# The second feed-forward stage token by token: its convolution as three shifted float32 products

## The reference, cut to what matters

```python
def act_quant(x):
    scale = 127.0 / clip(max(abs(x), axis=-1, keepdims=True), 1e-5)
    return clip(round(x * scale), -128, 127) / scale
def bit_linear(x, w):       # w becomes -1, 0 or 1 times its mean absolute value
    return einsum('bsd,hd->bsh', act_quant(x), weight_quant(w))
h = bit_linear(layernorm(x), w1)            # 128 -> 512
h = depthwise_conv1d(h, conv_w, conv_b)     # three taps along the tokens of a sequence
h = silu(h)
x = x + tanh(g_ffn[1]) * bit_linear(h, w2)  # 512 -> 128
```

## Time and profile before

| | us |
|---|---|
| median of three runs | 1844.87 |
| lowest and highest | 1843.51, 1848.87 |
| span of the profiled execution | 1861.1 |
| stage F1 in it, first statistics to last residual | 527.0 to 712.45 |

### The profile page before, as it was taken

The page is one execution under the profiler, slowest core; times in us unless marked ns, Lnnn a source line. Parts: engine busy times, 40 slices in busy tenths (PEclk is TensorE's granted clock), DMA queues, the critical chain, the costliest instruction groups (busy, mean ns, idle before and its releaser), DMA issues.

```text
span 1861.1 us, 35910 instructions
## 1 busy us (share of the span) xinstructions
PE 1404.8 (75%) x9844; PEld 1054.7 (57%) x9844; DVE 1333.1 (72%) x4156; ACT 1024.2 (55%) x2876; POOL 492.1 (26%) x499
## 2 busy tenths in 40 slices
PE   3677776987734446676769998989997409999995
PEld 3455554665523334433325666666666408999995
DVE  3888886888879986889945667766766455666665
ACT  3677785432425553311037777767785326777773
POOL 5433530221100001100000032232233333555451
PEclk9999998999965557978789999999999758999998
DMA  7000069300199910000000000000000052222226
GB/s 167 7 7 6 12 83 160 48 0 1 34 145 157 162 18 17 28 1 0 1 6 1 7 26 22 16 29 23 10 23 24 27 223 61 64 66 68 64 64 227
DMA packets 144711, 97.75 MB, mean 53 GB/s; under 512 B 21658, under 2 KB 133934, under 8 KB 143443
## 3 DMA queue, kind: packets, MB, share of 16 engines
q1 hardware_dynamic: 135890, 79.49, 23.2%
q0 software_dynamic: 8704, 16.87, 2.8%
HBM read 42.43 MB, written 54.93 MB: 52 GB/s over the span
## 4 chain that ended last, share of the span: by engine, by line
PE 36%; issue 31%; DVE 17%; ACT 9%; POOL 2%; DMA 1%; SPq 1%; another core or an unknown queue 1%; DVEq 1%; ACTq 0%; POOLq 0%
PE bank L1227 6%; PE bank L1219 6%; PE bank L863 5%; PE bank L912 3%; PE bank L879 3%; ACT att L1383 2%; ACT arena L1260 2%; PE bank L899 2%; PE bank L889 2%; DVE nm L1699 2%; PE bank L867 2%; DVE att L1700 1%; DVE tmp L1977 1%; DVE arena L1843 1%
## 5 line engine op out<-in xcount | busy, mean ns | idle before, releaser
L1260 ACT ACTIVATE arena<-bank 128x512 f32<-128x512 f32 (+6 forms) x440 | 255.5, 614 | 141.2 <-PE bank L1083 61.5
L540 POOL TENSOR_TENSOR rstd<-ve,mhalf 128x4 f32<-128x4 f32 x64 | 67.0, 1046 | 688.2 <-DVE ve L1680 688.2
L1383 ACT ACTIVATE att<-bank,arena 128x128 f32<-128x128 f32 x512 | 181.5, 377 | 81.8 <-DVE arena L1843 79.9
L1615 ACT ACTIVATE att<-bank,arena 128x128 f32<-128x128 f32 x576 | 164.6, 371 | 69.9 <-PE bank L1219 67.6
L639 POOL DMA_INDIRECT dispatched_rows<-arena x128 | 132.5, 1035 | 222.0 <-DVE arena L1761 153.5
L690 POOL DMA_INDIRECT expert_outputs<-arena x144 | 144.7, 1005 | 148.1 <-issue 102.9
L1260 ACT ACTIVATE xnT<-bank 128x128 f32<-128x128 f32 (+1 forms) x180 | 63.4, 352 | 190.2 <-PE bank L711 134.8
L1227 PE MATMUL bank<-arena,att 128*128 128x128 f32 x1152 | 154.1, 277 | 3.0 <-ACT att L1615 1.9
L1219 PE MATMUL bank<-xnT,arena 128*128 128x128 f32 x1152 | 154.1, 277 | 0.2 <-ACT xnT L1260 0.2
L1227 PEld LDWEIGHTS bank<-arena,att 128*128 128x128 f32 x1152 | 141.0, 193 | 5.3 <-ACT att L1615 5.3
L1219 PEld LDWEIGHTS bank<-xnT,arena 128*128 128x128 f32 x1152 | 141.6, 194 | 0.8 <-ACT xnT L1260 0.8
(11 more groups left out here) (324 smaller groups left out, 3306.1 us busy)
## 6 DMA issues: line engine op xcount, KB each, us to landing
dispatched_rows<-padf SPq DMA_DIRECT2D x16, 2128.5 KB, 35.4
arena<-dispatched_rows SPq DMA_DIRECT2D x144, 64.5 KB
cxT<-in_ctx SPq DMA_DIRECT2D x32, 256.0 KB, 2.7
arena<-in_L_ffn_w SPq DMA_DIRECT2D x8, 1024.0 KB
arena<-expert_outputs SPq DMA_DIRECT2D x8, 1024.0 KB, 13.7
expert_outputs<-arena POOLq DMA_INDIRECT x144
dispatched_rows<-arena POOLq DMA_INDIRECT x128
out_x<-x SPq DMA_DIRECT2D x8, 256.0 KB, 4.8
```

What stands on the lines that cost most here:

```text
L1260: copy = lambda o, i: nc.scalar.activation(o, i, ACT.Copy)
L1383: last = nc.scalar.activation(ex3_of(w, side)[:, i, :], bank[side][:, i * P:i * P + P], ACT.Exp, bias=nm3[:, w % 2, h:h + 1], accum_out=su ...
L1615: last = nc.scalar.activation(h3[:, s % 2, k * P:k * P + P], bank[s % 2][:, k * P:k * P + P], ACT.Gelu, bias=b1c3[:, s % 4, k:k + 1])
```

## The change

F1 now keeps the hidden values token by token. The quantised input of a token is an integer times its scale, so the change multiplies them together before the product (`xs1`, on GpSimd), transposes that in float32 (`spread`) into a tile with one zero column at either end of each sequence (`xsT1`, two chunks deep), and lets the convolution run inside the product: for each sequence three float32 products with the tile shifted by 0, 1 and 2 columns, each with its own weights `wconv1[:, t, :]` (ternary weight times tap times weight scale), all in one bank, ahead of them a bf16 product of three rows that adds the bias. The four steps `scaled`, `middle`, `taps` and `tokens_back`, the spread of the scales and their transposes and copy go. ScalarE's SiLU reads PSUM. The maxima, factors, rounding, integers, transposes, copy and second product are done sequence by sequence; TensorE's transposes of the integers and the second product stand three sequences (`LAG1`) behind the first one. The rounding of the input moves from VectorE to ScalarE (`rounded_x`). The order in each engine's program is that of the loops over j below.

In the set-up, GpSimd makes `wconv1` and `cbias1` after its last `split` of A0. The loads of the taps and the bias have other shapes, 128 partitions of 6 KB and three of 2 KB in place of 512 pieces of 12 bytes and 512 of 4. The semaphores of the set-up become one (`s_setup`, whose values are GATES to WEIGHTS), as do three of F3's routing and two of F0; the order of their work stays.

The core of the diff, without its common indentation. Removed lines of F1 stand in the functions printed above and are left out; a line without a sign is unchanged. The blocks are, after the tiles and loads: GpSimd's set-up, GpSimd in F1, TensorE, ScalarE, VectorE.

```diff
+LAG1 = 3
...
+wconv1 = ar([P, 3, H1])
+cb1, cbrest1 = ar([3, H1]), ar([3, H1])
+cbpart1 = [ar([3, H1], BF16) for _ in range(3)]
+cbias1, ones3 = ar([3, H1], BF16), ar([3, P], BF16)
+xr1, xq1, xs1 = ar([P, CB, P]), ar([P, CB, P]), ar([P, CB, P])
+xsT1 = ar([P, 2 * CB, P + 2])
...
-(cw1[:, :, :], a["L1_ffn_conv_w"].rearrange("(k p) a t -> p k (a t)", p=P)),
-(cb1[:, :], a["L1_ffn_conv_b"].rearrange("(k p) -> p k", p=P)),
+(wconv1[:, :, :], a["L1_ffn_conv_w"].rearrange("(a t) h -> a t h", a=1)[0].partition_broadcast(P)),
+(cb1[:, :], rows(a["L1_ffn_conv_b"], 3)),
...
+pl.wait_ge(s_load, 16 * n_loads)
+rest = cb1
+for i in range(3):
+    step(pl.tensor_copy(cbpart1[i][:, :], rest[:, :]))
+    if i < 2:
+        step(pl.tensor_tensor(cbrest1[:, :], rest[:, :], cbpart1[i][:, :], ALU.subtract))
+    rest = cbrest1
+for i in range(3):
+    step(pl.tensor_scalar(cbpart1[i][:, :], cbpart1[i][:, :], ident[0:3, i:i + 1], None, ALU.mult))
+step(pl.tensor_tensor(cbias1[:, :], cbpart1[0][:, :], cbpart1[1][:, :], ALU.add))
+pl.tensor_tensor(cbias1[:, :], cbias1[:, :], cbpart1[2][:, :], ALU.add).then_inc(sem("F1_constants"), 1)
+pl.memset(ones3[:, :], 1.0).then_inc(sem("F1_constants"), 1)
+pl.wait_ge(s_setup, WEIGHTS)
+for t in range(3):
+    step(pl.tensor_tensor(wconv1[:, t, :], wconv1[:, t, :], w1q[:, :], ALU.mult))
+    pl.tensor_scalar(wconv1[:, t, :], wconv1[:, t, :], wsc1[:, 0:1], None, ALU.mult).then_inc(sem("F1_constants"), 1)
...
+stage_start(pl, STAGE["F1"])
+pl.memset(xsT1[:, :, 0:1], 0.0).then_inc(sem("F1_edges"), 1)
+pl.memset(xsT1[:, :, P + 1:P + 2], 0.0).then_inc(sem("F1_edges"), 1)
 with pl.Fori(0, NC) as c:
     power("F1", c)
-    pl.wait_ge(sem("F1_scale1"), c + 1)
-    pl.wait_ge(sem("F1_scaleT"), c + 1)
-    pl.sem_inc(s_held, 1)
-    pl.tensor_copy(iscb1[:, :, :], am1[:, :].unsqueeze(2).to_broadcast([P, CB, P])).then_inc(sem("F1_scale_spread"), 1)
+    pl.wait_ge(sem("F1_xq"), c + 1)
+    pl.wait_ge(sem("F1_xsT_full"), c + 1)
+    pl.tensor_tensor(xs1[:, :, :], xq1[:, :, :], am1[:, :].unsqueeze(2).to_broadcast([P, CB, P]), ALU.mult).then_inc(sem("F1_xs"), 1)
...
+def spread(c):
+    pe.wait_ge(sem("F1_xs"), c + 1)
+    pe.wait_ge(sem("F1_xsT"), c + 1)
     for j in range(CB):
+        last = nc.tensor.transpose(bank[0][:, j * P:j * P + P], xs1[:, j, :], ident[:, :])
+    last.then_inc(sem("F1_xsT_full"), 1)
+def up(c, p, j):
+    if j == 0:
+        pe.wait_ge(sem("F1_xsT"), c + 2)
+    pe.wait_ge(sem("F1_silu"), c * CB + (j + 1))
+    nc.tensor.matmul(bank[1 + j][:, :], ones3[:, :], cbias1[:, :], start=True, stop=False)
+    for t in range(3):
+        last = nc.tensor.matmul(bank[1 + j][:, :], xsT1[:, p * CB + j, t:t + P], wconv1[:, t, :], start=False, stop=(t == 2))
+    last.then_inc(sem("F1_up"), 1)
+def integers_T(c, j):
+    pe.wait_ge(sem("F1_hq"), c * CB + (j + 1))
+    pe.wait_ge(sem("F1_hqT"), c * CB + (j + 1))
     for k in range(K1):
+        last = nc.tensor.transpose(bank[5 + j % 2][:, :].bitcast(BF16)[:, k * P:k * P + P], hq1[:, j, k * P:k * P + P], ident16[:, :])
+    last.then_inc(sem("F1_hqT_full"), 1)
+def down(c, j):
+    pe.wait_ge(sem("F1_hqT"), c * CB + (j + 3))
+    if j == 0:
+        pe.wait_ge(s_xdone, c + (NC * STAGE["F1"] + 1))
+    for k in range(K1):
+        last = nc.tensor.matmul(bank[7][:, j * P:j * P + P], hqT1[:, j % 2, k * P:k * P + P], w2q[:, k, :],
+                                start=(k == 0), stop=(k == K1 - 1))
+    last.then_inc(sem("F1_y"), 1)
+def f1(c, p, more, first=False, live=True):
+    for j in range(CB if live else LAG1):
+        before = (c, j - LAG1) if j >= LAG1 else None if first else (c - 1, j - LAG1 + CB)
+        if before:
+            integers_T(*before)
+        if live:
+            up(c, p, j)
+            if j == 2 and more:
+                spread(c + 1)
+        if before:
+            down(*before)
+pe.wait_ge(sem("F1_constants"), 5)
+pe.wait_ge(sem("F1_edges"), 2)
+spread(0)
+f1(0, 0, True, first=True)
+with pe.Fori(0, NC // 2 - 1) as i:
+    for p in range(2):
+        f1(i * 2 + (p + 1), 1 - p, True)
+f1(NC - 1, 1, False)
+f1(NC, 0, False, live=False)
...
+def spread(c, p):
+    act.wait_ge(sem("F1_xsT_full"), c + 2)
+    if not isinstance(c, int) or c > 1:
+        act.wait_ge(sem("F1_up"), c * CB - CB)
+    copy(xsT1[:, p * CB:p * CB + CB, 1:1 + P], b4(0)).then_inc(sem("F1_xsT"), 1)
+def rounded_x(c):
+    act.wait_ge(sem("F1_scale1"), c + 1)
     for j in range(CB):
+        last = rnd(xr1[:, j, :], xn[:, j, :], sc1[:, j:j + 1])
+    last.then_inc(sem("F1_xr"), 1)
+def rounded_h(c, j):
+    act.wait_ge(sem("F1_scale2"), c * CB + (j + 1))
+    rnd(hr1[:, j, :], hs1[:, j, :], sc2[:, j:j + 1]).then_inc(sem("F1_round2"), 1)
+def integers_T(c, j):
+    act.wait_ge(sem("F1_hqT_full"), c * CB + (j + 1))
+    act.wait_ge(sem("F1_y"), c * CB + (j + 1))
+    copy(hqT1[:, j % 2, :], bank[5 + j % 2][:, 0:H1 // 2].bitcast(BF16)).then_inc(sem("F1_hqT"), 1)
+def f1(c, p, more, first=False, live=True):
+    for j in range(CB if live else LAG1):
+        before = (c, j - LAG1) if j >= LAG1 else None if first else (c - 1, j - LAG1 + CB)
+        if before:
+            integers_T(*before)
+        if live:
+            act.wait_ge(sem("F1_up"), c * CB + (j + 1))
+            nc.scalar.activation(hs1[:, j, :], bank[1 + j][:, :], ACT.Silu).then_inc(sem("F1_silu"), 1)
+        if live and j == 1 and more:
+            rounded_x(c + 1)
+        if live and j == 3 and more:
+            spread(c + 1, 1 - p)
+        if j == 0 and not first:
+            rounded_h(c - 1, CB - 1)
+        if live and j:
+            rounded_h(c, j - 1)
+rounded_x(0)
+spread(0, 0)
+f1(0, 0, True, first=True)
+with act.Fori(0, NC // 2 - 1) as i:
+    for p in range(2):
+        f1(i * 2 + (p + 1), 1 - p, True)
+f1(NC - 1, 1, False)
+f1(NC, 0, False, live=False)
...
+def f1_apply(c, first):
     norm_apply("F1", c, xc(c), ready=False)
     if not first:
+        dve.wait_ge(sem("F1_xs"), c)
     step(v.tensor_reduce(am1[:, :], xn[:, :, :], AX, ALU.max, apply_absolute_value=True))
     step(v.tensor_scalar(am1[:, :], am1[:, :], EPS, None, ALU.max))
     step(v.reciprocal(sc1[:, :], am1[:, :]))
     v.tensor_scalar(sc1[:, :], sc1[:, :], 127.0, None, ALU.mult).then_inc(sem("F1_scale1"), 1)
+def f1_integers(c):
+    dve.wait_ge(sem("F1_xr"), c + 1)
+    v.tensor_scalar(xq1[:, :, :], xr1[:, :, :], ROUND, 127.0, ALU.subtract, ALU.min).then_inc(sem("F1_xq"), 1)
+def scales(c, p, j):
+    dve.wait_ge(sem("F1_silu"), c * CB + (j + 1 + CB))
+    step(v.tensor_reduce(am2[:, j:j + 1], hs1[:, j, :], AX, ALU.max, apply_absolute_value=True))
+    step(v.tensor_scalar(am2[:, j:j + 1], am2[:, j:j + 1], EPS, None, ALU.max))
+    step(v.reciprocal(sc2[:, j:j + 1], am2[:, j:j + 1]))
+    v.tensor_scalar(sc2[:, j:j + 1], sc2[:, j:j + 1], 127.0, None, ALU.mult).then_inc(sem("F1_scale2"), 1)
+    v.tensor_scalar(isc2[:, p, j:j + 1], am2[:, j:j + 1], wsc2[:, 0:1], gates[:, 5:6], ALU.mult, ALU.mult)
+def hq(c, j, first):
+    dve.wait_ge(sem("F1_round2"), c * CB + (j + 1))
+    if not first:
+        dve.wait_ge(sem("F1_hqT_full"), c * CB + (j + 1 - CB))
+    v.tensor_scalar(hq1[:, j, :], hr1[:, j, :], ROUND, 127.0, ALU.subtract, ALU.min).then_inc(sem("F1_hq"), 1)
+def residual1(c, p):
+    dve.wait_ge(sem("F1_y"), c * CB + CB + 2)
+    dve.sem_inc(s_held, 1)
     for j in range(CB):
+        last = v.scalar_tensor_tensor(xc(c)[:, j, :], bank[7][:, j * P:j * P + P], isc2[:, p, j:j + 1], xc(c)[:, j, :], ALU.mult, ALU.add)
     last.then_inc(s_xdone, 1)
+def f1(c, p, more, first=False, live=True, second=False, ahead=True):
+    for j in range(CB if live else LAG1):
+        if live:
+            scales(c, p, j)
+        if j == 0 and not first:
+            hq(c - 1, CB - 1, second)
+        if live and j:
+            hq(c, j - 1, first)
+        if live and more:
+            if j == 0:
+                f1_apply(c + 1, False)
+            if j == 1:
+                f1_integers(c + 1)
+            if j == 3 and ahead:
+                norm_stats(xc(c + 2))
+                norm_var("F1")
+        if j == 2 and not first:
+            residual1(c - 1, 1 - p)
 norm_stats(xc(0))
 norm_var("F1")
+f1_apply(0, True)
+f1_integers(0)
+norm_stats(xc(1))
+norm_var("F1")
+f1(0, 0, True, first=True)
+f1(1, 1, True, second=True)
+step.loop(2 * (3 * CB + 2 + 1 + 3))
+with dve.Fori(1, NC // 2 - 1) as i:
+    step.turn(i - 1)
+    for p in range(2):
+        f1(i * 2 + p, p, True)
+step.end(NC // 2 - 2)
+f1(NC - 2, 0, True, ahead=False)
+f1(NC - 1, 1, False)
+f1(NC, 0, False, live=False)
...
```

More of the change, by code:

```diff
@@ L34 @@
 E0, I0 = 4, 64
-MIDDLE1 = (1, 3)
+LAG1 = 3
 TAPS0 = 4
@@ L60 @@
 ARENA = 31000
+LATE = 24000
 SLICES0 = (0, 3, 4, 8, 11, 12, 13, 14)
@@ L1073, in _ @@
             stage_start(pe, STAGE["F1"])
-            b0h = bank[0][:, :].bitcast(BF16)
-            def up1(c, first):
-                pe.wait_ge(sem("F1_xq"), c + 1)
-                if not first:
-                    pe.wait_ge(sem("F1_hqT"), c * 2 - 1)
```

(85 more changed lines are left out.)

153 lines of the change are left out of this document (29 added, 124 removed).

## The result

The changed kernel takes **1828.7 us** (median of four runs, 1826.6 to 1832.7) against 1846.9 for the kernel before beside it: a ratio of 0.990, 95% interval 0.988 to 0.992. The forecast was 1830.0.

A forecast was written before the change was run, and what follows sets the result against it. VectorE bounded F1 before; afterwards TensorE and its feeding chain would. F1 of 18.5 + 7 x 19.4 + 16.1 = 170.4 us, 15.0 below 185.45, took 14.9 off 1844.87: 1830 us, range 1816 to 1850.

The forecast's parts named there:

- The bound moves off VectorE: In F1, VectorE keeps 11.5 of 19.4 us busy per chunk; TensorE and the chain feeding it bound instead.
- The float32 product: On TensorE in F1, one product of 512 columns takes about 0.87 us at full clock, 1.75 at half.
- The rival built on it: Float32 product cheaper than its records, 0.43 us: F1 147 us, time 1808; chance 0.05.
- The chain: In F1, dependent steps across engines from one chunk's first SiLU to the next's: pitch 18.1 us at full clock.
- TensorE's idle stretch: TensorE waits 3.0 us in each F1 chunk ahead of `spread`, with `up` of sequence 3 queued behind.
- The clock: TensorE's clock falls in two F1 chunks of three, holding back 2 us each: 1.3 on average, pitch 19.4.
- The ends: F1's filling takes 18.5 us and its draining 16.1 with some low clock.
- What costs nothing: GpSimd's set-up, at most 22 us, is covered by 47.02 us idle before F0; the larger load is also free.
- Other stages change by under 2 us: Sign against the prediction: it is wrong if any stage other than F1 changes by over 2 us.
- Full clock throughout: Rival: TensorE's clock never falls in F1; pitch 18.1, draining 15.1, F1 160.3 us, time 1820; chance 0.18.
- The slower case: Rival: low clock lasts after TensorE's wait ahead of `spread`; pitch 22.4, F1 191, time 1851, always low 1903; chance 0.15.
- no difference: Rival: the slower mechanism at break-even, F1 pitch between 20.75 and 22.3 us, time 1845; chance 0.12.

The follow-up runs named there:

- The double product: The changed kernel with GpSimd making the product by the scales a second time, into a spare buffer: 1844.0 us, ratio 0.998 to the kernel before.
- the last experiment: Changed kernel with later transposes of scaled input, later input rounding on ScalarE, and VectorE's residual and input integers ahead of sequence 2's maxima: 1804.7 us, ratio 0.977.
- the 128-row products: The changed kernel with five thrown-away products, 128 x 128 stationary operand, in TensorE's idle stretch: 1826.9 us, ratio 0.989 to the kernel before.

## Why the prediction was right

**The bound moves off VectorE: right.** 19.35 to 11.7 us of a chunk (11.5 forecast), ScalarE 9.3 (near 10).

**The float32 product: right.** A product, two records, was to take 0.87 us and took 0.89: the six records of a sequence take 2.68, from 577.20 to the next product at 579.88. (The rows had 0.89 too, as the difference of 1.91 and 1.02.) `up` takes 3.00 us (3.0), though by other parts: the bias product 0.32 where I took 0.2, and no 0.2 of latency. The Trainium skill's page "Perfetto Trace Analysis" (Engine Utilization) halves the rate for FP32_LOW_HIGH; it doesn't say that a plain float32 product is meant, and if it is, the 0.89 us disagree here too. The rival built on it is out.

**The chain: right, link by link.** From the end of SiLU of sequence 0 (567.3):

| | forecast | measured |
|---|---|---|
| input rounded | 5.8 | 5.9 |
| hidden values of sequence 0 rounded | 6.6 | 6.6 |
| both sets of integers | 7.4 | 7.4 |
| product on GpSimd | 8.8 | 8.5 |
| `up` of sequence 3 begins, ends | 10.0, 13.0 | 9.6, 12.6 |
| copied | 14.4 | 13.8 |
| next `up` ends (584.30) | 17.4 | 17.0 |
| SiLU | 18.1 | 17.8 |

The one link off is GpSimd's product, 1.04 us where F0's of the same size had 1.26.

**TensorE's idle stretch: right in place, too long.** 2.1 to 2.2 us (2.65 in the first chunk) for 3.0: `up` of sequence 2 ended at 6.4, not 5.9, as I had left out the second product and transposes between, and the product came 0.3 earlier.

**The clock: right in kind.** It fell in every second chunk, four times, at 1.7 us each, where I had 2 us in two of three. Pitch 18.7 for 19.4, granted clock 0.90 over F1 (0.75 to 1.00).

**The ends: one right, one wrong by 1.6.** Filling took 16.9 us, not 18.5: I had put ScalarE's table load on the path, and it ran at 542.01, while TensorE was in the first `up`. Draining took 16.7 (16.1). So F1, from the first statistics to the end of the last residual, is 16.9 + 7 x 18.7 + 16.7 = 164.5 us where I had 170.4.

**What costs nothing: right for F0.** It lasts 144.1 us after A0 where it had 143.8, with 17.6 us more on GpSimd between 250 and 320 us; the last of the new constants is done at 291.7. The double product shows what such work costs where it isn't covered.

**Other stages change by under 2 us: wrong.** The prediction had named this as a sign against itself. A1 and A2 took 2.7 and 3.1 more. In A1 the granted clock is lower, before (second profile) and after (second profile):

```profile
461.90:530.10 68.20, 47.07 (x256) 0.90 0.19 47
```

```profile
461.30:532.20 70.90, 50.73 (x256) 0.84 0.20 48
```

This is no matter of single executions: F0 and A1 together take 211.9 and 212.1 us in the two profiles of the kernel before and 214.5 to 215.1 in all eleven of changed kernels. What in the change shifts the clock there is open. For A2 TensorE's clock at its start shows it, before (second profile) and after (second profile), 9 to 18 us behind the last residual:

```profile
725.20:728.20 3.00, 3.00 (x16) 0.62 0.00 0
728.20:731.20 3.00, 0.96 (x9) 1.00 0.29 87
731.20:734.20 3.00, 3.00 (x16) 1.00 0.00 0
```

```profile
706.30:709.30 3.00, 3.00 (x13) 0.50 0.00 0
709.30:712.30 3.00, 1.33 (x11) 0.97 0.30 87
712.30:715.30 3.00, 2.62 (x4) 0.60 0.03 8
```

After the change the clock rose later and fell once more. For A2 it isn't the code: with the same program of A2 it took 66.2 us again in the last experiment (granted clock 0.91, against 0.86 in the changed kernel's second profile) and 66.3 without the bias product. Which of the two starts comes seems to hang on where the clock stands when a stage ends; that was not tried by itself.

So the forecast of 1830 is closer than its parts, because two errors partly cancel, and that is luck: F1 came out 5.9 us shorter than forecast, and A1, A2 and F3 together gave 3.2 back, which the prediction had at nothing. (Up to its last residual F3 differs by 6.3 us between the two profiles of the kernel before, so its share can't be put to the change.)

**The rivals.** Full clock throughout did not come, but the 128-row products show it was near: F1 160.5. The slower case never came into reach in the changed kernel; the doubled product is its mechanism (a longer wait at `spread`, the clock down in every chunk) and ended at no difference, at a pitch of 20.6. The 1903 us given for a clock that is always low need ends 8 us longer than the 34.6 of the sum, which the prediction didn't work out.

## What to carry to other kernels

When a change moves work from a full engine to an idle one, write out the chain of one period with the times of its links, and look for an in-order queue that holds ready work behind a late operand: here `up` of sequence 3 stood behind `spread`, and moving one call was worth nearly as much in F1 (20.3 us) as the change itself (21.0). Count for each engine what lag its program allows between a result and the instruction that waits for it; one step too few closed a ring here (1951 us in place of 1830). Check the neighbouring stages, and profile the kernel before twice, before a difference of spans is put down to a change.
